# Two softmaxes of an audio tower: the heads' maxima subtracted on VectorE, one exponential over all heads on ScalarE

## The reference, cut to what is computed

```python
h = tok(x)                # depthwise conv, 192x192 matmul, relu, max over token pairs (62 tokens left), fft2, layernorm
h = h + attn0(ln(h))      # 8 heads, relative positions: softmax(content + rel) @ v, output 768 -> 192
h = h + ffn(ln(h))        # gated, rows quantised to 8 bits ahead of both matmuls, ternary weights
h = h + attn1(ln(h))      # 12 heads in 3 groups of 4 that share a key and a value head, rotary, T = 62
h = h + moe(ln(h))        # 8 experts, each token goes to one
```

## Time and profile before

| what | value |
|---|---|
| median of 3 runs | 1205.06 us (1203.88 to 1205.45) |
| the profiled execution | 1207.81 us, span 1205.9 us |
| busy share of the span | PE 83%, ACT 70%, DVE 66%, POOL 31% |
| loop period, from the start of one f_yq to the next | 27.73 us, 26 times in a row within 0.01 us |
| first phase ends, experts begin | at about 1010 us of the span |

### The profile page before, as it was taken

One profiled execution on the slowest core, in us unless ns is written; L12 is line 12 of the kernel. 1 busy time (PEld: TensorE's weight loads), 2 busy tenths in 40 slices (PEclk: granted clock), 3 DMA queues, 4 the chain that ended last, 5 costly groups with the idle time before them and its releaser, 6 DMA issues. The chain is left out here.

```text
span 1205.9 us, 31213 instructions
## 1 busy us (share of the span) xinstructions
PE 1004.8 (83%) x9406; PEld 761.8 (63%) x9439; DVE 792.0 (66%) x2641; ACT 838.8 (70%) x2673; POOL 368.1 (31%) x1100
## 2 busy tenths in 40 slices
PE   3658988999899999898998999999888541999996
PEld 2436666666666666666666666666666421888885
DVE  2355777777777777777777777777775422555553
ACT  1436888888888888888888888888887420333332
POOL 2012333333333333333333333333332211122222
PEclk9987999999999999999999999999999655999998
DMA  6135111111111111111111111111111007122221
GB/s 217 33 118 156 33 40 39 38 45 38 38 38 55 43 48 38 38 38 38 39 43 38 38 44 49 48 43 38 38 33 33 12 20 212 49 58 56 56 61 39
DMA packets 73487, 65.62 MB, mean 54 GB/s; under 512 B 39341, under 2 KB 63696, under 8 KB 73328
## 3 DMA queue, kind: packets, MB, share of 16 engines
q1 hardware_dynamic: 63232, 46.43, 12.9%
q0 software_dynamic: 4512, 12.52, 3.2%
q10 hardware_dynamic: 5712, 6.29, 1.8%
HBM read 36.57 MB, written 28.95 MB: 54 GB/s over the span
## 5 line engine op out<-in xcount | busy, mean ns | idle before, releaser
L1192 DVE SCALAR_TENSOR_TENSOR conv_lo<-xT_lo,c_taps,conv_lo 128x248 f32<-128x248 f32 x192 | 89.8, 468 | 20.4 <-ACT xT_hi L901 20.4
L1137 ACT ACTIVATE e_tanh<-bank_a 128x512 f32<-128x512 f32 x34 | 20.3, 597 | 93.4 <-PE bank_a L590 93.4
L1087 ACT ACTIVATE p<-bank_b,max 128x62 f32<-128x62 f32 x384 | 81.1, 352 | 0.0
L499 POOL TENSOR_TENSOR var_y<-ssq_y,c_eps 128x1 f32<-128x1 f32 x32 | 6.1, 192 | 235.3 <-ACT f_sq L1057 235.3
L590 PE MATMUL bank_a<-e_xT,w_now 128*128 128x128 f32 x544 | 70.5, 284 | 7.5 <-DVE e_gate L1467 3.4
L590 PEld LDWEIGHTS bank_a<-e_xT,w_now 128*128 128x128 f32 x544 | 64.9, 196 | 16.7 <-issue 11.0
L590 PE MATMUL bank_a<-c_wv,a_xT 64*64 64x384 f32 (+1 forms) x512 | 74.0, 503 | 0.0
L590 PE MATMUL bank_a<-a_xT,c_wq 64*128 64x128 f32 (+1 forms) x512 | 71.7, 282 | 0.0
L1462 DVE COPY w_now<-w_sb 128x512 f32 x34 | 14.5, 427 | 83.9 <-PE bank_a L590 74.6
L590 PE MATMUL bank_a<-a_xT,c_wk 64*128 64x128 f32 (+1 forms) x512 | 69.2, 281 | 0.0
L590 PE MATMUL bank_a<-c_wo,oT 128*128 128x192 f32 x384 | 68.5, 329 | 0.5 <-ACT oT L901 0.4
(11 more groups left out here) (264 smaller groups left out, 3006.7 us busy)
## 6 DMA issues: line engine op xcount, KB each, us to landing
rel_scores<-rel_tok SPq DMA_DIRECT2D x32, 492.0 KB, 2.6
rel_skew<-rel_scores SPq DMA_DIRECT2D x64, 124.0 KB, 3.0
x_tok<-in_x SPq DMA_DIRECT2D x32, 187.5 KB
e_rest<-routed SPq DMA_DIRECT2D x34, 97.0 KB
e_tok<-routed SPq DMA_DIRECT2D x34, 96.0 KB, 1.9
routed<-pad_rows SPq DMA_DIRECT2D x8, 386.0 KB, 2.8
w_sb<-in_w ACTq DMA_DIRECT2D x1, 3072.0 KB, 12.4
w_sb<-in_w ACTq DMA_DIRECT2D x2, 1024.0 KB, 14.7
```

What stands on the lines that cost most here:

```text
L499: pool.tensor_tensor(out=var[k][:, :], in0=ssq[k][:, :], in1=c_eps[:, width:width + 1], op=ALU.mult).then_inc(var_eps[k], 1)
L1087: last = nc.scalar.activation(p1[:, h, 0:T], src[:, at * T:(at + 1) * T], ACT.Exp, bias=max1[:, mx:mx + 1])
L1137: nc.scalar.activation(e_tanh[:, :], pa0[:, :], ACT.Tanh, scale=0.5).then_inc(e_tanhr, 1)
L1192: c.mark(v.scalar_tensor_tensor(conv_lo[:, :, :], xT_lo[:, :, k:k + PAIRS], c_taps[:, 0, k:k + 1], conv_lo[:, :, :], ALU.mult, ALU.add))
```

## The change

Each maximum is followed on VectorE by an addition of the negated maxima, broadcast over the 62 keys, that reads the scores in PSUM and writes them into the buffer of the probabilities; ScalarE then takes one exponential in place over all heads. `b` needs two additions, one for each bank. New are also the waits that guard them: for the maxima just written (`c.link`, `c.wait`), and for the transposes of the tile before, which must have read `p0` or `p1` (`after_previous(dve, a_pt, m)` and `b_pt`). ScalarE's exponentials lose their bias operand.

```diff
             def a_expo(m):
                 act.wait_ge(a_shift, m + 1)
-                for h in range(H0):
-                    last = nc.scalar.activation(p0[:, h, 0:T], pa1[:, h * T:(h + 1) * T], ACT.Exp, bias=max0[:, h:h + 1])
-                last.then_inc(a_exp, 1)
+                nc.scalar.activation(p0[:, :, 0:T], p0[:, :, 0:T], ACT.Exp).then_inc(a_exp, 1)
...
             def b_expo(m):
                 act.wait_ge(b_shift, m + 1)
-                for h in range(H1):
-                    src, at = (pb1, h - REP) if REP <= h < 2 * REP else (pb0, h if h < REP else h - REP)
-                    mx = 2 * REP + at if src is pb1 else at
-                    last = nc.scalar.activation(p1[:, h, 0:T], src[:, at * T:(at + 1) * T], ACT.Exp, bias=max1[:, mx:mx + 1])
-                last.then_inc(b_exp, 1)
+                nc.scalar.activation(p1[:, :, 0:T], p1[:, :, 0:T], ACT.Exp).then_inc(b_exp, 1)
...
             def a_max_scores(m):
+                c = ch["a"]
+                c.stage("max", m)
                 dve.wait_ge(a_s, m + 1)
-                v.tensor_reduce(max0[:, :], pa1[:, 0:H0 * T].rearrange("p (h s) -> p h s", h=H0), axis=AX.X,
-                                op=ALU.max, negate=True).then_inc(a_shift, 1)
+                scores = pa1[:, 0:H0 * T].rearrange("p (h s) -> p h s", h=H0)
+                c.link(v.tensor_reduce(max0[:, :], scores, axis=AX.X, op=ALU.max, negate=True))
+                after_previous(dve, a_pt, m)
+                v.tensor_tensor(p0[:, :, 0:T], scores, max0[:, :].unsqueeze(2).broadcast_to([P, H0, T]),
+                                ALU.add).then_inc(a_shift, 1)
...
             def b_max_scores(m):
+                c = ch["b"]
+                c.stage("max", m)
                 dve.wait_ge(b_s, 4 * m + 4)
-                for src, lo, n in ((pb0, 0, 2 * REP), (pb1, 2 * REP, REP)):
-                    last = v.tensor_reduce(max1[:, lo:lo + n], src[:, 0:n * T].rearrange("p (h s) -> p h s", h=n),
-                                           axis=AX.X, op=ALU.max, negate=True)
-                last.then_inc(b_shift, 1)
+                outer = pb0[:, 0:2 * REP * T].rearrange("p (h s) -> p h s", h=2 * REP)
+                middle = pb1[:, 0:REP * T].rearrange("p (h s) -> p h s", h=REP)
+                c.mark(v.tensor_reduce(max1[:, 0:2 * REP], outer, axis=AX.X, op=ALU.max, negate=True))
+                c.mark(v.tensor_reduce(max1[:, 2 * REP:H1], middle, axis=AX.X, op=ALU.max, negate=True))
+                after_previous(dve, b_pt, m)
+                groups = p1[:, :, :].rearrange("p (g h) s -> p g h s", g=KV1)
+                c.wait(back=1)
+                v.tensor_tensor(groups[:, 0:KV1:2, :, 0:T], outer.rearrange("p (g h) s -> p g h s", g=2),
+                                max1[:, 0:2 * REP].rearrange("p (g h) -> p g h", g=2).unsqueeze(3).broadcast_to([P, 2, REP, T]),
+                                ALU.add)
+                c.wait()
+                v.tensor_tensor(groups[:, 1, :, 0:T], middle, max1[:, 2 * REP:H1].unsqueeze(2).broadcast_to([P, REP, T]),
+                                ALU.add).then_inc(b_shift, 1)
```

## The result

The changed kernel takes 1212.66 us (median of 7 runs, 1207.53 to 1219.12), the kernel before beside it 1205.02: a ratio of 1.0075, 95% interval 1.0046 to 1.0104. It is slower by 0.75%, where 0.22% was forecast; the median lies just inside the range, whose upper end was 1213.0. The profiled execution took 1218.22 us with a span of 1216.4; it is the second slowest of the seven.

What follows compares the result with a forecast made beforehand. The loop was taken as bound by the chain through VectorE's maximum, stats_t and quantisation to f_yq; +4.6 in the loop and -0.3 - 0.3 - 0.6 - 0.7 at the ends made +2.7, 1207.8 us, range 1201.5 to 1213.0.

Steps and rivals of the forecast that it cites:

- The path: Loop: f_yq, the feed-forward's rounded activations, paces it; TensorE's wait for it grows from 0.63 to about 1.1 us.
- The wait for p: TensorE, first attention's probabilities: wait ends 0.3 us earlier, addition 0.71 plus exponential 0.71 replacing 1.73; 0.35 to 0.4 left.
- rival 1: ScalarE's backlog holds f_yq, so the 0.3 us won on p reaches the period: 1194.5 us; chance 0.16.
- The additions of `b`: VectorE, second attention: two additions fit the 1.02 us gap before f_gate, with 0.18 us of room; cost nothing.
- Rival 2: VectorE: additions of `b` don't overlap, f_gate comes 0.14 us late each iteration: +6.8, 1211.9 us; chance 0.22.
- The addition of `a`: VectorE, first attention: 0.62 us of work meets 0.46 idle before stats_t; the scale comes 0.16 us later.
- Neither is worth anything in the loop: Earlier z_sb (`t_dft_seq` up to 0.2 us earlier) and f_sq (0.55 earlier) gain nothing in the loop.
- All that follows f_yq shifts with it: Loop, up to the next scores: period 27.73 + 0.16 = 27.89 us over 29 iterations, +4.6 us.
- The exponentials: ScalarE: one instruction per attention, 0.71 us for 496 elements and 0.91 for 744, taken from the rounding rows.
- the 0.3 us off the sum: By the skill page's shorter exponentials, 0.60 and 0.81 us, the sum would be 0.3 us lower, all in the last iterations.
- The ends: Iterations 2, 33, 34 and 35, outside the loop: shorter latency gives -0.3, -0.3, -0.6 and -0.7 us.

Runs made afterwards that it cites:

- e2_a_only: Only the first attention's half of the change (`a_expo`, `a_max_scores`), the second as before, against the kernel before: ratio 1.0062.
- e12_after_again: The changed kernel, unaltered, run again on the chip of the later runs, against the kernel before: ratio 1.006.
- e4_q_first: VectorE's quantisation of y moved ahead of `t_moments`, against the changed kernel; measured beside the kernel before: ratio 1.0257.

## Why the prediction was right or wrong

**The path, right.** f_yq paces the loop, and what is won ahead of it only makes the wait longer: the wait for f_yq rose to 1.18 (forecast 1.0 to 1.1). The wait for p came down only from 0.70 to 0.60, where 0.35 to 0.4 was forecast. The forecast had moved the end of that wait and not its start: with z_sb early TensorE is there 0.3 us sooner, and in e2_a_only, where z_sb is late, the wait is 0.29. ScalarE's relief (rival 1) brought nothing in the changed kernel, where 2.54 + 1.73 us of exponentials became 0.82 + 0.62.

**The additions of `b`, right.** They end 514.81 - 512.91 = 1.90 us after the first maximum begins; the forecast had 507.05 - 505.13 = 1.92. Tanh ends at 514.14 + 0.69 = 514.83 and f_gate follows 0.09 later, as it did before. The overlaps are 0.09 (513.50 + 0.41 against 513.82) and 0.08, though each addition waits for a maximum. Rival 2 did not happen: its +0.14 would have shown in the period.

**The addition of `a`, right in its size, and wrong in its reason.** Period 27.89 forecast, 27.88 measured; VectorE's busy time grew by 47 us, less than the 55 I had, and ScalarE's fell by 86 (838.8 to 752.5), where I had "well over 100": both were reckoned from durations, and those overlap. The step "Neither is worth anything in the loop" holds for the changed kernel only: the earlier z_sb is worth 0.31 us an iteration as soon as nothing else stands ahead of stats_t. I had priced the two halves only together, so I did not see that the kernel's best version was half of the change, and that `a`'s addition costs 0.46, not 0.16, of what could be had.

**What failed: the sum took TensorE's clock as given.** The step "All that follows f_yq shifts with it", 27.73 + 0.16 = 27.89 for each of 29 iterations, made the longer wait for f_yq worth its own length only, and no term stood for a fall of the clock. In the changed kernel TensorE at times falls to 1.2 GHz after this wait, and that costs 1.65 us each time: six times in the profile, 9.9 us, against +4.3 for the shift itself, and by the medians two or three times. With the wait filled the drops are gone and the ratio is 1.0031, which is the forecast's; with the delay doubled there are 19 of them, filled again none. I had read the granted clock, 1.00, and not asked what a growing wait of TensorE does to it. The lowest of the seven runs, 1207.53, lies where the forecast had the median. That the median still lies in the range is luck: the range reached up to 1213.0 for rival 2, which did not happen.

**The exponentials, too dear.** 0.62 and 0.82 us, where I took 0.71 and 0.91 from the roundings. The estimate by the Trainium skill's page "ScalarE: Activation LUTs" (section "What ACT_TABLE_LOAD costs"), 0.60 and 0.81, agrees to 0.02. It changed nothing in the loop. By that estimate I had put the 0.3 us off the sum all in the last iterations; a third of it belongs to iteration 2.

**The ends, not decided.** Forecast -1.9. All that lies outside the loop gave some -3.8 in the first profile, but some -1.8 in e12_after_again (1218.4 - 1205.9 = 12.5, less 9.9 and 4.3). What follows the last f_yq took 242.5 us in the one and 245.3 in the other, of the same kernel, and 245.4 before; the ends differ between executions by as much as was forecast.

What stays open: which iterations are hit. All of the change's iterations have the same waits, but the clock drops in one of three, and only up to 722 us; e2_a_only waits as long for f_yq and less for p (11.0 us in 30), and had two drops in its one profile, where the change had six in both of its own. The single run times of the change, 1207.53 to 1219.12, spread over as much as seven drops would make. Their mean granted clocks fit in the main, 0.949 in the fastest and 0.938 in the slowest run, but the kernel before has 0.945 to 0.953 without a drop in its profile, so they give no count; only profiled executions show it.

## What to carry to other kernels

Before a change that lets an engine wait longer, ask of TensorE not only how long, but what its granted clock does after it, and look for short stretches at the lower level in windows of 1 us: a mean over the run (0.942 against 0.947) shows little. In a hand-ordered pipeline price each half of a change on its own: an instruction that comes earlier may be worth nothing only because the other half stands in its way. And an engine that is 87% busy gives nothing back unless the instruction that it holds up is on the path, here a copy of 0.4 us that feeds the next matmul.

## What the runs showed of the hardware that was not expected

A wait of TensorE that grows by half a microsecond, from 0.63 to 1.18, can cost three times its growth (1.65) in the iterations where the clock falls, and with two or four matmuls of constants in it no profile had a drop. In e4_q_first the drops come behind a wait of 0.94 for another operand, with 0.31 for f_yq. At 1.2 GHz six transposes take 1.49 us for 0.82, and the matmuls behind them as much.

Exponentials of 62 elements with a bias column, out of PSUM, follow each other at (2.54 - 0.35) / 11 = 0.20 us; those in place without it at (1.84 - 0.24) / 11 = 0.15 (241 ns is the mean of one). Behind exponentials without a bias z_sb and f_sq are shorter in the rows as well, 0.31 to 0.33 and 0.62 us instead of 0.42 and 0.73. For z_sb that is overlap: it ends 0.21 us after the last exponential with a bias (509.28 + 0.42 against 506.95 + 2.54), and 0.22 after the last one without (503.51 + 0.31 against 501.76 + 1.84). What makes the overlap longer behind exponentials with a bias, no run here shows.
